# The turning of the next tile placed behind the up products, late weight units in groups of two, and two moves in the attention's end and the second router

## What is computed

```
x = x + tanh(g_xattn[0]) * L0_attention(layernorm(x), ctx)      # sigmoid scores, 16 heads
x = x + tanh(g_ffn[0])   * L0_experts(layernorm(x))             # softmax router, top 2 of 8, and a shared expert
x = x + tanh(g_xattn[1]) * L1_attention(ctx, layernorm(x))      # linear attention with its own layernorm
x = x + tanh(g_ffn[1])   * L1_experts(layernorm(x))             # top 2 of 8, softmax over the two
# an expert: h = gelu(x @ W1e + b1e);  y = h @ W2e + b2e        # 256 -> 1024 -> 256
```

## Time and profile before

| | |
|---|---|
| median of three runs | 714.69 us |
| the profiled execution | 718.92 us, span of its core 716.5 us |
| PE busy | 94% of the span |
| mean granted clock of PE | 0.977 |
| 270 to 414 us (first loop) | PE busy 142.7 of 144 us |
| 130 to 160 us (attention's end) | PE busy 26.8 of 30 us |
| 465 to 478 us (second router) | granted clock 0.50 |

### The profile page before, as it was taken

One profiled execution on the slowest core, in us unless ns is written; L12 is line 12 of the kernel. 1 busy time (PEld: TensorE's weight loads), 2 busy tenths in 40 slices (PEclk: granted clock), 3 DMA queues, 4 the chain that ended last, 5 costly groups with the idle time before them and its releaser, 6 DMA issues.

```text
span 716.5 us, 21813 instructions
## 1 busy us (share of the span) xinstructions
PE 672.2 (94%) x7522; PEld 574.9 (80%) x7523; DVE 473.8 (66%) x1188; ACT 464.7 (65%) x1178; POOL 297.5 (42%) x221
## 2 busy tenths in 40 slices
PE   4898999989988999999999989999999999999992
PEld 4433667679878999998999979776999999999992
DVE  4899787847668776765664569965997454454541
ACT  2476787745478877776866637941997656656561
POOL 1101153534715565455555323402365555545432
PEclk9999999999999999999999999869999999999997
DMA  8981101327086857789876479944544444444531
GB/s 267 374 291 43 26 16 45 84 64 254 30 283 184 179 108 168 192 206 265 197 178 114 74 204 414 371 172 126 156 88 75 81 81 74 79 75 69 79 50 23
DMA packets 110679, 104.97 MB, mean 147 GB/s; under 512 B 53067, under 2 KB 96085, under 8 KB 109734
## 3 DMA queue, kind: packets, MB, share of 16 engines
q1 hardware_dynamic: 95654, 83.80, 37.8%
q0 software_dynamic: 14976, 20.58, 17.7%
HBM read 64.84 MB, written 28.23 MB: 130 GB/s over the span
## 4 chain that ended last, share of the span: by engine, by line
PE 76%; DVE 9%; ACT 5%; DMA 3%; issue 3%; POOL 2%; SPq 0%; POOLq 0%; ACTq 0%; DVEq 0%
PE bank L1265 9%; PE bank L1263 9%; PE bank L1264 9%; PE bank L1276 9%; PE bank L1278 9%; PE bank L1277 9%; PE bank L1384 2%; DVE weights L1820 2%; PE bank L998 2%; DMA out<-x_arena,add_now 1%; PE bank L1151 1%; PE bank L955 1%; POOL weights L840 1%; PE bank L1170 1%; PE bank L1153 1%
## 5 line engine op out<-in xcount | busy, mean ns | idle before, releaser
L1587 ACT ACTIVATE work<-bank,b_cols 128x128 f32<-128x128 f32 x624 | 176.1, 383 | 135.5 <-PE bank L1265 132.4
L1263 PE MATMUL bank<-x_arena,weights 128*128 128x128 f16 x1248 | 213.2, 219 | 1.4 <-DVE x_arena L2072 0.7
L1264 PE MATMUL bank<-x_arena,weights 128*128 128x128 f16 x1248 | 213.1, 219 | 0.0
L1265 PE MATMUL bank<-x_arena,weights 128*128 128x128 f16 x1248 | 213.1, 219 | 0.0
L2087 DVE TENSOR_TENSOR work<-work 128x512 f16<-128x512 f32 x156 | 101.0, 689 | 127.8 <-ACT work L1595 116.9
L1276 PE MATMUL bank<-weights,work 128*128 x624 | 170.2, 273 | 2.1 <-issue 1.4
L1277 PE MATMUL bank<-weights,work 128*128 x624 | 170.1, 273 | 0.0
L1278 PE MATMUL bank<-weights,work 128*128 x624 | 170.1, 273 | 0.0
L846 POOL DMA_INDIRECT x_arena<-token_rows,gather_now x78 | 85.0, 1089 | 149.1 <-DVE gather_now L2081 103.6
L1263 PEld LDWEIGHTS bank<-x_arena,weights 128*128 x1248 | 122.1, 98 | 2.4 <-DVE x_arena L2072 1.1
L1264 PEld LDWEIGHTS bank<-x_arena,weights 128*128 x1248 | 122.1, 98 | 1.2 <-issue 0.4
(11 more groups left out here) (249 smaller groups left out, 1211.8 us busy)
## 6 DMA issues: line engine op xcount, KB each, us to landing
weights<-in_L_ffn_W SPq DMA_DIRECT2D x76, 256.0 KB, 7.4
raw<-in_L_ffn_W SPq DMA_DIRECT2D x44, 256.0 KB
split_dram<-row_arena SPq DMA_DIRECT2D x12, 512.0 KB
weights<-split_dram SPq DMA_DIRECT2D x3, 2048.0 KB, 16.9
odd_sum<-padding_row SPq DMA_DIRECT2D x1, 2176.0 KB, 13.4
token_rows<-row_arena SPq DMA_DIRECT2D x1, 2072.0 KB, 7.6
x_arena<-in_x SPq DMA_DIRECT2D x4, 512.0 KB, 6.4
weights<-in_L_ffn_sW SPq DMA_DIRECT2D x8, 256.0 KB, 7.6
```

Source lines behind the costliest of these rows:

```text
L1263: nc.tensor.matmul(o, w1_at[f][c][0].block(), hi, start=c == 0, stop=False)
L1264: nc.tensor.matmul(o, w1_at[f][c][0].block(), lo, start=False, stop=False)
L1265: m = nc.tensor.matmul(o, w1_at[f][c][1].block(), hi, start=False, stop=c == DC - 1)
L1587: m = nc.scalar.activation(hid[:, k, f * P:f * P + P], h_ps[k][half][:, g * P:g * P + P], ACT.Gelu, bias=b1_cols[n][:, f, bass.ds(e, 1)], ...
```

## The change

It has four parts; the four functions are the only ones touched.

1. In the first loop PE's body j is, for j = 1 to 4, `up(j)`, `turn(j + 1)`, `down(j - 1)`. For j = 0 the turn stays ahead.
2. SP's late units: 24 and 25 at the routing's end; 26, 27 after the rows of tile 3; 28, 29 after tile 4; 30, 31 after tile 5, then 32; 33 and 34 behind the transfer of tile 6; 35 and layer 1's unit 0 behind tile 7, its unit 1 behind tile 8.
3. ACT's `rows(3)` stands behind `shared_high(16)` instead of `shared_high(15)`.
4. In the second router three products of 512 columns stand ahead of the first logits, and one behind every second pair of logits products and behind each half: 3 + 4 x 4 = 19 more.

```diff
-            for u in range(24, 28):
+            for u in range(24, 26):
                 load_unit(0, u)
             sp.wait_ge(rows_stored[0], 16)
             for j in range(3, 6):
                 sp.wait_ge(row_in[j % 2][0], 16 * (j // 2 + 1))
-                if j == 5:
-                    sp.wait_ge(s_down_done, STEPS)
-                for u in range(22 + 2 * j, 24 + 2 * j):
+                for u in range(20 + 2 * j, 22 + 2 * j):
                     load_unit(0, u)
+            sp.wait_ge(s_down_done, STEPS)
+            load_unit(0, 32)
...
                 if j == 6:
-                    for u in range(34, 36):
+                    for u in range(33, 35):
                         load_unit(0, u)
                 if j == 7:
-                    for u in range(2):
-                        split_done(sp, 0, 18 + u)
-                        load_unit(1, u)
+                    load_unit(0, 35)
+                if j in (7, 8):
+                    split_done(sp, 0, 11 + j)
+                    load_unit(1, j - 7)
...
-                    if isinstance(j, int) and on_tensor(n, j + 1):
+                    turns_next = isinstance(j, int) and on_tensor(n, j + 1)
+                    if turns_next and j == 0:
                         turn(j + 1, q + (1 if k else 0), 1 - k)
                     up(j, q, k)
+                    if turns_next and j:
+                        turn(j + 1, q + (1 if k else 0), 1 - k)
...
             def router_logits1(b, h):
+                if (b, h) == (0, 0):
+                    keep_clock(bank[7], 3)
                 pe.wait_ge(router_xlnT_ready, half_no(b, h))
...
                     for c in range(DC):
                         m = nc.tensor.matmul(logits1_ps(i)[:, 0:E], ...)
+                        if t % 2 == 0 and c == DC - 1:
+                            keep_clock(bank[7], 1)
                 m.then_inc(xlnT_used, 1)
+                keep_clock(bank[7], 1)
...
                     shared_high(m)
-                    if m == IN_ATTENTION:
+                    if m == IN_ATTENTION + 1:
                         rows(3)
```

## The result

| | median | executions | lowest to highest |
|---|---|---|---|
| before | 715.31 us | 15 | 712.03 to 717.25 |
| changed | 708.67 us | 15 | 705.47 to 714.18 |

The ratio is 0.9916 (95% interval 0.9897 to 0.9935), 6.6 us off the median. The forecast was 708.5.

What follows compares the result with a forecast made beforehand. PE, carrying 76% of the chain, was taken as the bound. Loop 2.7, attention 1.5 and router 2.0 sum to 6.2 us, taken off the median 714.69 for 708.5; forecast 706.8 to 710.0, whole range 704.8 to 713.0.

Steps and rivals of the forecast that it cites:

- three places: The first loop's start, the attention's end and the second router, where the change touches PE's timeline.
- First loop, 2.7 us: Turns behind the up products let up(5) start at 225.2 instead of 227.88; 2.7 us won, bounds 0.5 and 4.5.
- the forecast's 208.37: First loop: the time DVE's copy of tile 2 is done, whatever PE does, letting up(2) start at 208.4.
- the second wait: First loop: PE's wait of 2.46 us in front of the turning of tile 4, ended by gathered rows landing.
- the whole rest of the loop, which is bound by PE, moves with it: First loop: the 2.7 us won at up(5) carry through all later bodies.
- the thinnest cover: First loop: tile 6's transposing transfer, wanted by up(6) at 230.5, with its rows gathered near 220.
- the next wait takes the loop's gain: Rival: late rows of tile 4 or 6, or late units; loop gives 0.5 us, 710.7 in all; chance 0.08.
- The smaller groups: First loop: two units fewer ahead of tile 4's gather, which should land some 3 us after its issue.
- Attention's end, 1.5 us: Gelu 16 runs in ACT's idle time, the last batch's logits come earlier; 1.5 us won, bounds 0.5 and 2.5.
- Second router, 2.0 us: Wide products hold full clock most of the way; 2.0 us won, bounds 3.8 won and 7.8 lost.
- all holds: Rival: router 3.8, attention 2.5, loop 2.7, together 9.0 us, giving 705.7; chance 0.15.
- The worked price if it holds: Second router: first logits to DVE's read of the counts takes 20.6 us instead of 24.4 at full clock.

Runs made afterwards that it cites:

- e3_att: The kernel before with only ACT's rows(3) moved behind step 16: ratio 0.9994, 713.57 us.
- e1_loop: The kernel before with only the first loop's parts, the turn behind the up products and SP's units in smaller groups: ratio 0.9999, 714.49 us.
- r2_fewer: The changed kernel with 11 of the 19 wide router products, none within a half: ratio 0.9949, 711.38 us.
- b1_no_sp: The changed kernel with SP's queue as before, all else kept: ratio 0.9896, 708.82 us.
- r1_blocks: The changed kernel with the same 19 wide router products in blocks, none among the small ones: ratio 0.9958, 711.68 us.
- a2_no_router: The changed kernel with the second router as before, without the wide products: ratio 0.9946, 712.49 us.

## Why the prediction was right, and where it was not

The total was right (6.2 us forecast, 6.6 measured), but in part by luck: a loop term that was too large (2.7 against 0.8) was made up by a router term that was too small (2.0 against 4.2 by the distances, 2.0 to 3.3 by the times). By its own steps:

- **Reading the profile.** That PE bounds the kernel and that there are three places held. What failed was to take one execution as the kernel: the sum was made against 718.92 us and laid on the median, as if the 4.2 us between them lay outside the three places. By the distances 1.1 us of it had come by up(5) of the first loop, and 1.9 by up(9).
- **First loop, 2.7 us.** The waits of the earlier trace rows went, and the turn fits between up(1) and down(0). Up(0) to up(5) takes 25.72 us, 2.8 less than in the undisturbed traces of the old loop (28.53 on average), as forecast (2.4 less on the average of the eight new ones, 26.18). That DVE's copies stay where they are, whatever PE does, held too: tile 2's begins 8.42 us after up(0) in the changed kernel and 8.43 in e3_att. But the forecast's 208.37 was the late execution's, so the shares came out by luck: up(2) gained 1.7 us against e3_att, where 0.5 were forecast, and the second wait the rest, where 2.2 were. The step that failed is "the whole rest of the loop, which is bound by PE, moves with it": between up(5) and up(9) the eight traces lose 1.6 us against 4 x 5.30 on average (0.5 to 2.6), and 0.8 us are kept to up(9). What stood in its place are transfers that are issued and land no earlier than before: the rows of tiles 6 to 8 with their transposing transfers, and one entry ahead in DVE's queue the scattered adds, which the text did not cost. Tile 6's transfer, which it called the thinnest cover and gave as a sign of being wrong, did hold up(6), by 0.28 us in the changed kernel, 1.26 in e1_loop and 1.05 in r2_fewer. That is the rival "the next wait takes the loop's gain", which names the rows of tile 6, at nearly its price (0.5 us); it had a chance of 0.08.
- **The smaller groups.** The landing of tile 4's rows came at 5.5 us after the gather's issue, not at 3, and it was not needed: b1_no_sp.
- **Attention's end, 1.5 us.** 1.86 measured, in every trace. The steps held one by one: no wait at up(18), one of 0.79 us, the normalising 0.76 us longer (0.9 estimated from the earlier trace rows). The Trainium skill's page "SBUF — State Buffer", section "Who interferes with whom", says that of the two engines whoever issues first gets the shared port pair for the whole instruction, and the other is blocked. The trace agrees: one DVE instruction of 0.41 us became 1.17 and ended 0.15 us behind POOL's, which had begun 0.14 us before it. The Trainium skill says this of DVE's modes that use both ports, and no trace shows the mode of the normalising.
- **Second router, 2.0 us.** The mechanism was right and the weight wrong: it was set at half of "all holds". The clock held throughout in four of seven traces and fell once, for some 3 us, in three; 4.2 us are won against the 3.8 of the full price, by the runs' times 2.0 to 3.3. The worked price if it holds, 20.6 us from the first logits to the read of the counts, was 1.2 too long: with the clock at 1.00 it is 19.4 to the end of the counts, and 20.7 to 21.0 with one fall. The Trainium skill's page "TensorE: Matmul & The Clock Gate", section "Part 4: PE-mode transpose", was weighed as speaking against the change. The three falls stand 1.1 to 1.9 us behind the turn of batch 2 and 0.86 us of idle time, which would fit it; no run parts the turn from the idle time, and four traces with the same stretch have no fall.
- **The parts together.** 0.8 + 1.9 + 4.2 = 6.9 us by the distances, 6.6 by the medians of the whole. The parts alone give 2.5 us by their ratios (0.9999, 0.9994 and 0.9972) and 6.3 by their medians, with intervals wide enough that both can hold; whether the parts help one another stays open. The attention's 1.9 us rest on the distances alone.

## What to carry to other kernels

Here a wait removed early in the pipeline paid only up to the next transfer whose issue and landing stayed where they were, so list every engine's waits in the bodies behind it, also those that now end just before anyone asks. One profiled execution is one draw: of the 3.9 us between two traces in the loop's first bodies 1.1 were that draw, and a part worth 1 us is told by stage distances, not by medians. Where the clock was at half among small products, wide ones spread among them held it here and the same number in blocks did not.

## What the runs showed of the hardware

- The granted clock can fall while PE is fully busy: in r1_blocks it fell at 462.6 us, in a window of 5 us with PE busy 5.00, while six wide products ran. In a2_no_router it fell in a window with PE busy 3.77 of 5. In both it then stayed at 0.50 with PE busy 5.00 of 5 us.
- The place of the fall differs between executions of the same router: distances of 21.7 to 26.0 us in five kernels that don't differ there. With all 19 products among them four of seven traces are at 19.42, the others 1.2 to 1.6 us above.
- A scattered add took 7.8 us (218.66 to 226.44) and 9.1 us from its issue to the release of its waiter, with weight transfers beside it; eight gathers in the changed kernel's first loop landed 3.7 to 6.7 us after their issue, against 2.8 us at the second loop's start.
- A DVE instruction that met one of POOL was held until 0.15 us behind POOL's end (0.41 became 1.17 us), and the three behind it and POOL's own kept their length.
- The time ahead of the attention's end is not fixed either: the last projection's logits stand 161.72 to 163.44 us from the start in four kernels that don't differ up to there.
